# Two-layer network on one core: gathers as transposes, stacks by groups, projections moved, maxima six steps ahead, and four output banks in the second layer

## The reference

```python
# layer 0: attention with binarised weights, 16 heads of 8
q, k, v = split_heads(binlinear(xn, Wq, bq)), ...
att = softmax(einsum('bhtd,bhsd->bhts', q, k) * Dh ** -0.5)
s = binlinear(merge(einsum('bhts,bhsd->bhtd', att, v)), Wp, bp)
# layer 0: mixture of 8 experts, best 2 of each token, and a shared one
f = sum_of_top2(w_e * ((silu(x @ w_gate[e]) * (x @ w_up[e])) @ w_down[e])) + shared(x)
# layer 1: causal attention with the Taylor feature map, 16 heads of 8, features of 16
A = tril(einsum('bhnd,bhmd->bhnm', taylor_exp(q), taylor_exp(k)))
s = (einsum('bhnm,bhme->bhne', A, v) / sums) @ Wo.T
# layer 1: three cycles of a coupling net (gelu MLP 128-128-64-32-1) and a context net
for _ in range(3):
    tf = sigmoid(gelu(gelu(gelu(out @ w1 + b1) @ w2 + b2) @ w3 + b3) @ w4 + b4)
    out = out + (0.1 + adaptive_range * (0.7 * gf + 0.3 * tf - 0.5) * 2) * twist(out)
```

## Time and profile before

| | us |
|---|---|
| median of 3 runs (lowest, highest) | 935.24 (933.85, 936.38) |
| the profiled execution | 927.35 |
| its span, first to last instruction | 925.2 |
| around the span | 2.15 |
| attention0 loop, from first score | 47.65 to about 409 |
| mixture of experts | 410.7 to 588.8 |
| second layer, coupling | 590.7 to 690.4 |
| second layer, attention | 690.4 to 925.2 |

### The profile page before, as it was taken

The page is one execution under the profiler, slowest core; times in us unless marked ns, Lnnn a source line. Parts: engine busy times, 40 slices in busy tenths (PEclk is TensorE's granted clock), DMA queues, the critical chain, the costliest instruction groups (busy, mean ns, idle before and its releaser), DMA issues. The chain is left out here.

```text
span 925.2 us, 17952 instructions
## 1 busy us (share of the span) xinstructions
PE 854.6 (92%) x6642; PEld 459.3 (50%) x6642; DVE 642.2 (69%) x949; ACT 628.0 (68%) x1216; POOL 387.9 (42%) x376
## 2 busy tenths in 40 slices
PE   4699999999999999979989989789879999999997
PEld 2333444444444344449889878432224444454554
DVE  6879988898888989514333338858696666666754
ACT  3669888888888988843323322357758878888885
POOL 4113140315454443105665642135655666656500
PEclk9579999999999999989999999979969999999999
DMA  7705726141423000126776653139996999999930
GB/s 238 275 25 229 254 66 234 56 156 45 167 89 122 29 26 28 57 55 199 222 209 204 186 181 110 27 72 146 144 126 71 101 123 119 110 119 123 123 40 23
DMA packets 81481, 114.07 MB, mean 123 GB/s; under 512 B 14482, under 2 KB 58516, under 8 KB 78964
## 3 DMA queue, kind: packets, MB, share of 16 engines
q1 hardware_dynamic: 74228, 94.68, 50.6%
q0 software_dynamic: 6352, 17.86, 5.7%
q10 hardware_dynamic: 816, 0.39, 0.1%
HBM read 56.07 MB, written 33.57 MB: 97 GB/s over the span
## 5 line engine op out<-in xcount | busy, mean ns | idle before, releaser
L1035 DVE TENSOR_REDUCE a_nmax<-quad 128x2 f32<-128x1024 f32 x256 | 301.5, 1213 | 41.0 <-PE quad L623 40.9
L813 ACT ACTIVATE a_probs<-bank 128x512 f32<-128x512 f32 x334 | 188.3, 603 | 26.1 <-PE misc L636 14.1
L1918 ACT ACTIVATE a_late<-quad 128x512 f32<-128x512 f32 x320 | 163.9, 613 | 25.3 <-PE quad L1687 25.3
L653 PE MATMUL av<-a_probs,a_va 128*32 128x256 f32 x2048 | 163.0, 391 | 7.8 <-ACT a_osb L820 7.2
L2078 DVE SCALAR_TENSOR_TENSOR a_late<-a_late,const 128x1024 f32<-128x1024 f32 (+1 forms) x80 | 98.2, 1229 | 73.2 <-ACT a_late L1918 73.2
L636 PE MATMUL bank<-q_stack,k_stack 25*128 25x512 f32 x334 | 138.5, 500 | 1.1 <-DMA q_stack<-a_ntop 0.9
L623 PE MATMUL quad<-k_stack,q_stack 24*128 24x512 f32 x512 | 132.1, 517 | 4.7 <-DVE a_nmax L1035 2.8
L813 ACT ACTIVATE a_probs<-misc 128x512 f32<-128x512 f32 x178 | 107.4, 603 | 13.9 <-PE bank L636 10.3
L1398 DVE TENSOR_TENSOR m_hid<-m_act,quad 128x512 f32<-128x512 f32 x55 | 37.4, 684 | 82.5 <-PE quad L1327 79.8
L636 PEld LDWEIGHTS bank<-q_stack,k_stack 25*128 25x128 f32 x334 | 55.0, 183 | 78.0 <-issue 48.6
L510 POOL DMA_INDIRECT sorted_rows<-x_rows,a_slot x64 | 62.4, 976 | 68.4 <-PE av L653 64.7
(11 more groups left out here) (317 smaller groups left out, 1400.4 us busy)
## 6 DMA issues: line engine op xcount, KB each, us to landing
spread<-a_parts SPq DMA_DIRECT2D x48, 256.0 KB
q_stack<-a_parts SPq DMA_DIRECT2D x96, 128.0 KB, 6.7
k_stack<-a_parts SPq DMA_DIRECT2D x96, 128.0 KB, 7.2
wu<-packed_weights SPq DMA_DIRECT2D x20, 384.0 KB, 3.3
m_wu<-packed_weights SPq DMA_DIRECT2D x19, 384.0 KB, 3.3
q_stack<-spread SPq DMA_DIRECT2D x7, 1024.0 KB, 4.9
k_stack<-spread SPq DMA_DIRECT2D x7, 1024.0 KB, 7.4
sorted_rows<-in_shape_constants POOLq DMA_DIRECT2D x5, 1040.0 KB, 6.4
```

The lines of the kernel that those rows point to most:

```text
L653: last = pe.matmul(av[STRIP * j:STRIP * (j + 1), at], va[b % 2][:, kt, GH * j + c, :], probs[:, (GH * s + j) % PROBS, at], start=(kt == 0 ...
L813: act.activation(probs[:, (GH * s + j) % PROBS, :], bank_of(n)[:, :], ACT.Exp, scale=scale).then_inc(unit_read, 1)
L1035: dve.tensor_reduce(nmax[quad % 2][:, at:at + 2 * TT:TT], max_pair(n), AX_X, ALU.max, negate=True).then_inc(max_free, 1)
L1918: act.activation(probs[:, (4 * ROUNDS * b + n) % 12, :], quad[:, n % 4, :], ACT.Square, bias=1.0, scale=0.25)\
```

## The change

In attention0: the gather becomes four transposes by the identity into strips of 32 (the selection matrix and its load go); the copy of the result, the inversion and the scaling read the strips. The stacks are read group by group, each pair behind a group's row transfers, and the spreads of q and k are issued apart. The q product moves from step 10 to step 2 of a batch (step 11 in batch 0) and the values from 14 to 10, both between the step's first scores and its first weighting; k stays at 12; the gathers move from 2 and 4 to 3 and 5, y from 6 to 7. AHEAD is 6, and a group is turned directly behind its last reduction. In second_layer: layer 4 has four banks, and its four passes follow one another; the context net uses `misc`; the last chunk's cast and split come behind the last update; the table of silu is loaded ahead; v is read in two parts, and weighting waits for the first.

```diff
-        gathered = sb("gathered", [P, 2, NCOMP])
+        gathered = sb("gathered", [P, 2, H, DH + 1])
...
-        AHEAD = 7
-        STACK = 16 * 2
+        AHEAD = 6
+        STACK = 16 * 2 * NG
...
-        GATHER_AT, TURN_AT, PROJECT_AT, QK_AT, VALUES_AT = (2, 4), 6, 8, (10, 12), 14
+        GATHER_AT, TURN_AT, PROJECT_AT, VALUES_AT = (3, 5), 7, 8, 10
...
+        def projected_at(b, t):
+            if b + LEAD >= B:
+                return ()
+            return ((0,) if t == (2 if b else 11) else ()) + ((1,) if t == 12 else ())
...
+        def stacked_by(b):
+            return STACK * (b // 2) + (16 * 2 if b % 2 == 0 else STACK) if b >= 0 else 0
...
+        def strips_of(n):
+            return bank_of(n).rearrange("p (k j h r) -> p k j h r", k=2, j=GH, h=2)
...
-            def stack(b):
+            def stack(b, c):
                 wait(sp, written, WRITES * (b + 1))
...
+                for op, dst in enumerate((qs, ks)):
+                    src = S["spread"][b % 2][op].rearrange("r n (d c) t -> (r n d) c t", d=DH)
+                    sp.dma_start(dst[b % 4][:, c, :], src[:, c, :]).then_inc(stacked[b % 2], 16)
...
-                    if b == 0 and c == 1:
-                        stack(LEAD - 1)
-                    if b >= 0 and c == 2 and b + LEAD < B:
-                        spread(b + LEAD, 0)
-                        spread(b + LEAD, 1)
-                    if b >= 0 and c == 3 and b + LEAD < B:
-                        stack(b + LEAD)
+                    if 0 <= NG * b + c - 1 < NG:
+                        stack(LEAD - 1, NG * b + c - 1)
+                    if b >= 1 and b - 1 + LEAD < B:
+                        stack(b - 1 + LEAD, c)
+                    if b >= 0 and c >= 2 and b + LEAD < B:
+                        spread(b + LEAD, c - 2)
...
                 for k in range(2):
                     t = 2 * u + k
                     for half in range(2):
-                        last = pe.matmul(bank_of(n)[:, k * NCOMP:(k + 1) * NCOMP], osb[b % 2][:, half, t * P:(t + 1) * P],
-                                         sel[:, half * NCOMP:(half + 1) * NCOMP], start=(half == 0), stop=(half == 1))
+                        last = pe.transpose(to[:, k, :, half, :], osb[b % 2][:, half, t * P:(t + 1) * P], S["ident"])
...
                 group(s, 0)
+                if t == 2:
+                    for op in projected_at(b, t):
+                        q_k(b + LEAD, op)
+                if t == VALUES_AT and b + 1 < B:
+                    values(b + 1)
                 if s >= LAG:
                     weigh(s - LAG, 0)
...
-                wait(act, split_q, min(b + LEAD + 1, B))
+                wait(act, split_q, min(b + LEAD + 2, B))
...
             def maxima(m):
                 maximum(m, 0)
-                if m % TT == 0 and m > 0:
-                    turn(m // TT - 1)
                 maximum(m, 1)
+                if m % TT == TT - 1:
+                    turn(m // TT)
...
+        def out_bank(n):
+            return (quad[:, 2, :], quad[:, 3, :], quad[:, 1, :], av[:, :])[n % GROUP]
...
-                    for c in EARLY[k][i:i + 1]:
+                    for c in EARLY[k][i:i + 1] if k < SLOTS else EARLY[k] if i else ():
                         split_one(c, c % 4)
...
-                wait(pe, lay[3], n - 1)
+                wait(pe, lay[3], n - 3)
...
                 if k >= 1:
-                    layer4(n - GROUP)
-                    layer4(n - GROUP + 1)
+                    for i in range(GROUP):
+                        layer4(n - GROUP + i)
                 if k == 1:
                     context_net(2)
...
-                if k >= 1:
-                    layer4(n - GROUP + 2)
-                    layer4(n - GROUP + 3)
                 if more:
                     layer2(2 * k + 1)
...
+            act.activation(ahead[:, :], S["ones"][:, 0:1], ACT.Silu)
             for i in range(B):
                 main(i, i % 2, i)
...
                     mask(i, u)
+                    if n == 0 and u == 0:
+                        read_v_heads(0, 0)
...
-                for c in EARLY[n // GROUP + 1][n // 2 % 2:n // 2 % 2 + 1]:
+                early, i = EARLY[n // GROUP + 1], n // 2 % 2
+                for c in early[i:i + 1] if n < ALL - GROUP else early if i else ():
                     cast(c // 4, c % 4)
```

More of the change, by code:

```diff
@@ L92, in shape_constants @@
     pad[:, :, IDCOL] = (TOPK * TOKENS + P * np.arange(PADS)[None, :] + np.arange(P)[:, None]).astype(np.int32).view(np.float32)
-    return np.concatenate([ident, tri, tri, ones, sel.reshape(P, -1), sign, lower, steps, pairs.reshape(P, -1), pad.reshape(P, -1)], axis=1)
+    return np.concatenate([ident, tri, tri, ones, sel.reshape(P, -1), sign, lower, steps, pad.reshape(P, -1)], axis=1)
 CONST_COLS = 4 * P + 2 * NCOMP + 1 + EXPERTS * EXPERTS + EXPERTS + MOST + ROOM
-PAIR_COLS = 2 * NCOMP
 def load_unit_rows(sp, S, u, to, done):
@@ L256, in attention0 @@
             b, t = s // 16, s % 16
-            units += [("s", s, j) for j in range(GH)]
+            units += [("s", s, 0), ("s", s, 1)]
+            units += [("qk", b + LEAD, op) for op in projected_at(b, t) if t == 2]
+            if t == VALUES_AT and b + 1 < B:
+                units.append(("v", b + 1, 0))
+            units += [("s", s, 2), ("s", s, 3)]
             if s in GATES_AT:
@@ L267, in attention0 @@
                 units.append(("y", b - 1, 0))
-            if t in QK_AT and b + LEAD < B:
-                units.append(("qk", b + LEAD, QK_AT.index(t)))
+            units += [("qk", b + LEAD, op) for op in projected_at(b, t) if t != 2]
             if t == PROJECT_AT and b >= 1:
@@ L367, in _ @@
             spread(0, 1)
-            stack(0)
+            stack_first()
             for n, name in enumerate(("Wq", "Wk")):
@@ L375, in _ @@
                 sp.dma_start(w1[:, 4 + n, :], io["L1_attn_" + name]).then_inc(loaded1, 16)
-            sp.dma_start(sel[:, :], io["shape_constants"][:, CONST_COLS:CONST_COLS + PAIR_COLS]).then_inc(sel_in, 16)
             spread(1, 0)
             spread(1, 1)
-            stack(1)
+            for c in range(NG):
+                stack(1, c)
             for b in range(-1, B):
@@ L767, in _ @@
                     turn_y(b - 1)
-                if t in QK_AT and b + LEAD < B:
-                    q_k(b + LEAD, QK_AT.index(t))
+                if t != 2:
+                    for op in projected_at(b, t):
+                        q_k(b + LEAD, op)
                 if t == PROJECT_AT and b >= 1:
@@ L773, in _ @@
                     count()
-                if t == VALUES_AT and b + 1 < B:
-                    values(b + 1)
                 if s >= LAG:
@@ L804, in read_v, with exps @@
                 act.activation(va[b % 2][:, :, 1::2, DH + 1:2 * DH + 1], got[:, :, 1::2, :], ACT.Copy).then_inc(unit_read, 1)
-            def exps(s):
-                for j in range(GH):
+            def exps(s, i):
+                for j in range(2 * i, 2 * i + 2):
                     n = unit_no["s", s, j]
@@ L921, in _ @@
                 b, t = s // 16, s % 16
-                exps(s)
+                exps(s, 0)
+                if t == 2:
+                    for op in projected_at(b, t):
+                        read_qk(b + LEAD, op)
+                if t == VALUES_AT and b + 1 < B:
+                    read_v(b + 1)
+                exps(s, 1)
                 if t == LAG - 1 and b >= 1:
@@ L939, in _ @@
                     read_y(b - 1)
-                if t in QK_AT and b + LEAD < B:
-                    read_qk(b + LEAD, QK_AT.index(t))
+                if t != 2:
+                    for op in projected_at(b, t):
+                        read_qk(b + LEAD, op)
                 if t == PROJECT_AT and b >= 1:
@@ L1495, in second_layer @@
         swapped = xc[:, :, :].rearrange("p (b t) c -> p b (t c)", b=B)
-        half = sb("half", [P, 5])
+        half, ahead = sb("half", [P, 5]), sb("ahead", [P, 1])
         means, context = sb("means", [C, B]), sb("context", [C, B])
@@ L1790, in layer3 @@
                 wait(pe, lay[2], k)
+                wait(pe, lay[3], GROUP * (k - 1) + 3)
                 for i in range(GROUP):
@@ L1974, in layer4 @@
                 wait(act, coupled, n - 1)
[L1975 removed]
+                act.activation(tf[n % 2], out_bank(n), ACT.Tanh, bias=half[:, 0:1], scale=0.5).then_inc(lay[3], 1)
             def context_net(step):
```

92 lines of the change are left out of this document (41 added, 51 removed).

## The result

The changed kernel takes 941.3 us in the median of 20 runs (932.7 to 952.0), the kernel before in the same comparison 935.8 (927.4 to 941.8). The ratio is 1.0058, its 95% interval 1.0029 to 1.0086: slower by some 5.4 us. I had forecast 922.2, a gain of 13.

The account below looks back on a forecast made before the run. TensorE, 92% busy, was taken to bound the kernel, sharing a rhythm with VectorE and ScalarE. First-layer gains 16.3 less 1.2 and 5.0, plus 2.9 in the second, took 13.0 off median 935.24: 922.2 us, range 912 to 931.

Parts of the forecast that it names:

- Step a: Head attention: gathers as four transposes instead of eight passes save 0.62 us each, 9.3 together (4.5 to 9.9).
- Step b: Head attention: moved q and values products fill TensorE's waits for the accumulator's copy, saving 5.5 us (2.5 to 6).
- Step c: Startup: six steps ahead means fewer maxima before the first score and an earlier first turn, saving 1.5 us (1.0 to 2.0).
- Step d: Head attention loop: later turns leave less time until first scores; one or two groups lose slightly, 1.2 us together (0 to 4).
- Step e: Head attention: smaller stack transfers delay k's spread, POOL's split of q and the scaling behind it, costing 5.0 us (0 to 10).
- Steps f and g: Second layer: first gate opens 3.8 us sooner; layer 4's four banks and pass order cost 0.9; net gain 2.9.
- The late turn: Rival, first scores of all 32 groups: VectorE turns a whole reduction later than counted, 16 us, 938; chance 0.04.
- the clock: Rival, head attention: gather transposes drop TensorE's clock to 1.2 GHz, 2 us a batch, 938; chance 0.02.
- batches 5 and 6: Sign in the head attention: these batches come out near 40.4 us; staying above 41.5 would show the forecast wrong.
- batch 3: Sign in the head attention: this batch comes out near 42 us.
- the waits for rows in groups 8 and 9 alone: Sign in the head attention: scores wait for their rows in these two groups only.
- many groups wait for their rows: Sign in the head attention that would show the forecast wrong: scores waiting for rows in many groups.

Follow-up runs that it names:

- everything mended: Changed kernel with seven steps ahead, POOL's split behind the scaling, POOL's transfers moved, first rows ahead of batch 1's stacks: 917.2 us, ratio 0.9823.
- both edits: Changed kernel with maxima seven steps ahead again and q's product at step 11 in every batch: 907.3 us, ratio 0.9825 to the kernel before.

## Why the prediction was wrong

**Step a**, the gathers as transposes, was right: 0.65 for one, 1.2 us a batch, 5.6 us alone by the medians (2.4 to 8.9) where I had 9.3 (4.5 to 9.9).

**Step b**, half right. The values' product fills its wait: with seven steps ahead and q at step 11 batches 5 and 6 are 1.7 shorter than before, of which 1.24 are the gathers and 0.5 this. q's does not: with everything mended batches 2 to 4 are only 0.2, 0.2 and 0.1 shorter with q at step 2 than with it at step 11, where I had 0.5. The term is 4, not 5.5.

**Step c** counted 1.5 for the first group, and the first exponential came 0.7 later. I had taken the 4.2 from turn to loaded weights, with rows that landed 3.7 behind the turn, over into a startup in which eight stack transfers are now issued up to 41.3, right ahead of the turn at 41.87: the rows took 6.3. With the first rows ahead of them it is 46.36, 1.95 sooner. With the old stacks, the lead alone gives 46.75.

**Step d is the one that failed.** I wrote: "After the change 5.35 - 1.3 = 4.05 at the least, so one or two groups lose 0.1 or 0.2", and priced it at 1.2 with a bound of 4. It was worth 13.6 us (ratios 0.9972 and 0.9825, with q at step 11) to 17 (1.0058 and 0.9872). Three things were missing. First, the lead is made of the steps ahead of a batch's first group, and from these the values' product went (0.9 to 1.0 of it, by the run with v at step 14): without their waits the first groups of a batch kept 3.5 to 4.2 from turn to first score, not the 4.8 that I would have got from 6.1, while group 23, which I took for the tightest, kept 4.6. Second, I compared with the 4.2 of the startup, where rows landed 3.7 behind the turn, and gave group 8 and 9 alone their traffic. The trace of before had the rule already: its rows of groups 8 and 9 took 7.0 and 6.6, and these are the ones where POOL starts a transfer 0.5 and 0.6 behind the turn. In all 16 profiles rows behind the startup land in 5.6 to 7.7 where such a transfer starts between 0.5 ahead of the turn and 1.9 behind it, in 3.9 to 6.4 where it starts 0.6 to 1.6 ahead, and in 3.5 to 4.6 where it starts 2.1 or more ahead or 2.4 or more behind. The change moved turn and transfer onto each other in group 4. Third, the wait is not its whole price.

**Step e** had the right chain, and its waits are near what I said: 1.99 and 1.62 in batches 2 and 4 with the long lead (I had 2.5 and 1.8), and 4.4 us in all by the ratios of the kernels with q at step 2 and 11, whose intervals overlap (their profiled loops differ by 11.1). With the short lead the same move was worth 8.0. But the spread took 6.4 from issue to landing in batch 4 of the changed kernel, not 3.9, for which I had only half of a 5.8 for six and an allowance that no row gives; the wait there was 4.26, and with the clock behind it the order of POOL's queue was worth 10.7, over my bound of 10. And I had not seen that a held POOL also shifts its transfers onto the rows.

**Steps f and g** had the right chain and were too small: 4.4 from the last tanh to the gate (3.8 forecast), the coupling loop lost nothing (0.9 forecast), and the profiles have 3 to 6 us where I had 2.9. The medians of the second layer's part alone don't settle the size.

**The rivals.** The late turn (938, chance 0.04) and the clock (938, chance 0.02) name the two halves of what happened, each with the wrong cause: not each group by a little, but few by much, and not the transposes, but the waits. I gave each a small chance by itself and never asked what the one does to the other. The Trainium skill, "TensorE: Matmul & The Clock Gate", part 4, "PE-mode transpose", says that a transpose does not count as busy like other work; in the kernel with both edits and in the one with everything mended all 16 gathers are transposes, and the clock is at 1.00 through batches 1 to 6. The same page's section "HAM oscillation — how this bites in real kernels" describes the pattern that the runs do show: TensorE waits for a transfer, and the work behind the wait runs cold. Here some waits of about 1 us, shorter than those of its example, had the same behind them.

Of my list of signs batches 5 and 6, the gather, the copy waits and the gate came about as named; batch 3 (45.2, not 42) and the waits for rows in groups 8 and 9 alone (they came at 4, 8 and 24) did not, and "many groups wait for their rows" was the wrong alarm, since three were enough.

## What to carry to other kernels

Where TensorE is busy without a break, price each new wait as the wait and a stretch at half clock behind it: here 4.2 us of waiting cost 8.7, though not every short wait had such a stretch behind it. Before a lead is shortened, work it out for each group from turn to use, with the work that the same change takes out of that window, and against the slowest landing in the trace and not the usual one. And of two transfers that can meet, find the order in the queue that keeps them apart, and what can delay that queue.

## What the runs showed that I had not expected

The granted clock fell to 0.50 behind waits of 0.7 to 4.8 us in a loop in which TensorE is otherwise busy without a break, and stayed there for 3.4 to 23.9 us, once (behind a wait of 0.77) for 30.7; behind other waits of 0.7 to 1.3 it did not fall at all. Twice it fell for 20 us in the loop's last group, where scores and weightings are left alone with ScalarE, each time behind a copy wait of 0.56. The same kernel spreads by 1 to 2%, and over the 20 runs of the changed kernel the time follows the mean clock of the run (0.953 in one of 932.9, 0.932 in one of 952.0).

Four row transfers of 2 KB each that land in 3.5 us in most groups take up to 7.7 beside a copy of 1 MB that another queue started just behind them. The Trainium skill, "DMA: Bandwidth & Descriptors", section "Queues, rings and completion order", says that each transfer engine takes turns between its queues; the rows' times beside POOL's transfers agree with that, and no run here tells it from another shared limit.
